# A first scan stage whose normalisation and projections move, pair by pair of time tiles, into the scan's own loop

## The reference, cut to what matters

```python
xn = (x - mu) * jax.lax.rsqrt(var + LN_EPS) * ln_w + ln_b
x_proj = jnp.einsum('bld,ed->ble', xn, in_proj_w)        # 512 outputs
x_ssm, gate = jnp.split(x_proj, 2, axis=-1)              # 256 and 256
A = -jnp.clip(jnp.exp(A_log), -10.0, -0.01)
# each step, for 256 channels x 16 states:
h = jnp.clip(h * A[None] + x_t[:, :, None] * Bm[None], -10.0, 10.0)
y = jnp.einsum('bid,id->bi', h, C)
out = (out_f + out_b) * 0.5 * jax.nn.silu(gate)
return jnp.einsum('bli,di->bld', out, out_proj_w)
```

## Time and profile before

| what | value |
|---|---|
| median of 3 runs | 1257.77 us (1256.69 to 1260.92) |
| time of the profiled execution | 1258.15 us |
| its span | 1256.3 us |
| mean granted TensorE clock | 0.911 |
| VectorE busy over the span | 1009.9 us (80%) |
| TensorE busy over the span | 1027.6 us (82%) |
| ScalarE busy over the span | 714.5 us (57%) |
| GpSimd busy over the span | 582.9 us (46%) |

### The profile page before, as it was taken

One profiled execution on the slowest core, in us unless ns is written; L12 is line 12 of the kernel. 1 busy time (PEld: TensorE's weight loads), 2 busy tenths in 40 slices (PEclk: granted clock), 3 DMA queues, 4 the chain that ended last, 5 costly groups with the idle time before them and its releaser, 6 DMA issues. The chain is left out here.

```text
span 1256.3 us, 22969 instructions
## 1 busy us (share of the span) xinstructions
PE 1027.6 (82%) x8295; PEld 739.2 (59%) x8295; DVE 1009.9 (80%) x2090; ACT 714.5 (57%) x1504; POOL 582.9 (46%) x895
## 2 busy tenths in 40 slices
PE   2999888456599999999999788492688888778696
PEld 1555544143499999999999657340233333536555
DVE  4699999964599888899897537877999999677575
ACT  3866755015466666666665253266677777247453
POOL 2100000002588888888885231010799999225360
PEclk9988988777799999999999979886799999969989
DMA  1000000002211112111100010000200000000001
GB/s 44 1 1 1 2 1 1 1 14 98 89 61 66 69 74 75 71 66 66 71 27 2 1 23 1 1 1 4 61 1 1 0 1 1 1 2 3 3 0 30
DMA packets 16849, 32.49 MB, mean 26 GB/s; under 512 B 5072, under 2 KB 11968, under 8 KB 16736
## 3 DMA queue, kind: packets, MB, share of 16 engines
q1 hardware_dynamic: 16736, 31.02, 7.2%
HBM read 30.10 MB, written 0.92 MB: 25 GB/s over the span
## 5 line engine op out<-in xcount | busy, mean ns | idle before, releaser
L2129 POOL TENSOR_TENSOR m_h_in<-m_dtu,m_bs 128x448 f32<-128x448 f32 x128 | 144.4, 1148 | 69.7 <-DVE m_dtu L2173 53.6
L2196 DVE TENSOR_TENSOR_SCAN m_hs<-msp_da,m_h_in 128x448 f32<-128x448 f32 x128 | 136.4, 1082 | 1.5 <-ACT msp_da L2156 0.8
L672 DVE SCALAR_TENSOR_TENSOR l0r_u<-l0r_u,l0r_a_col 128x1024 f32<-128x1024 f32 x110 | 136.9, 1294 | 0.6 <-ACT l0r_u L627 0.6
L1054 POOL TENSOR_TENSOR bl_sc<-bl_sc,bl_topall 125x1456 f32<-125x1456 f32 x32 | 105.3, 3290 | 59.4 <-ACT bl_topall L1216 59.3
L627 ACT ACTIVATE l0r_u<-l0rp_pu 128x512 f32<-128x512 f32 x224 | 112.0, 643 | 35.9 <-PE l0rp_pu L563 35.8
L2092 PE MATMUL msp_py<-m_hc,ident 128*128 128x448 f32 x256 | 117.2, 542 | 0.0
L766 POOL MEMSET bq_lT<- 128x256 f32 x1 | 0.3, 311 | 238.0 <-POOLq L107 238.0
L563 PE MATMUL l0rp_pu<-l0r_xs,l0r_eb 32*128 32x256 f32 x896 | 104.6, 434 | 4.8 <-ACT l0r_u L627 4.1
L1291 PE MATMUL bl_pS<-b_qw,bl_xcT 128*125 128x112 f32 x768 | 104.0, 278 | 0.0
L2147 ACT ACTIVATE m_bs<-msp_pb 128x448 f32<-128x448 f32 x128 | 69.2, 541 | 44.1 <-PE msp_pb L2076 42.5
L563 PEld LDWEIGHTS l0rp_pu<-l0r_xs,l0r_eb 32*128 32x128 f32 x896 | 71.6, 193 | 37.4 <-ACT l0r_u L627 28.2
(11 more groups left out here) (401 smaller groups left out, 2528.3 us busy)
## 6 DMA issues: line engine op xcount, KB each, us to landing
b_xc<-in_ctx SPq DMA_DIRECT2D x16, 750.0 KB
bl_more<-in_ctx SPq DMA_DIRECT2D x16, 750.0 KB
x_tm<-in_x SPq DMA_DIRECT2D x1, 896.0 KB, 6.0
cw_cT<-in_ctx_headT SPq DMA_DIRECT2D x1, 896.0 KB
out_dram<-x_tm SPq DMA_DIRECT2D x4, 224.0 KB, 2.5
w_up<-in_L_ffn_w SPq DMA_DIRECT2D x1, 512.0 KB, 4.2
w_down<-in_L_ffn_w SPq DMA_DIRECT2D x1, 512.0 KB, 5.4
l0s_win<-in_L_attn_in_proj_wT SPq DMA_DIRECT2D x1, 256.0 KB, 2.6
```

The costliest lines, as they stand in the source:

```text
L672: ve.scalar_tensor_tensor(state(c, i, r), prev, a_col[:, :], state(c, i, r), ALU.mult, ALU.add).then_inc(step_done, 1)
L1054: pool.tensor_tensor(sc[0:KP, n % 3, :, :], sc[0:KP, n % 3, :, :], over(topall[0:KP, n % 2, :].unsqueeze(1), [KP, KT + 1, QR]), ALU.subtra ...
L2129: pool.tensor_tensor(h_in[:, n % NU, :], dtu[:, half, cols], bs[:, n % NU, :], ALU.mult).then_inc(s["db"], 1)
L2196: ve.tensor_tensor_scan(hs[:, n % NU, :], da[:, n % 2, 0:CH], h_in[:, n % NU, :], 0.0, ALU.mult, ALU.add).then_inc(s["scan"], 1)
```

## The change

The input is loaded a second time, as 14 time tiles `xr` whose 128 partitions are four steps times 32 sequences, so that a tile is what a chunk needs. Each of these loads is four DMAs, one for each step of a tile: SP issues tiles 0 and 13 first; ScalarE's queue issues `lnw`, `win` and the other twelve tiles. `x_tm`, needed only by the stage's last part, is loaded behind tiles 0 and 13. The block of constants, the first block of loads, `stage_norm` ahead of the scan and the block of preparations are gone: everything up to the scan's end is one block.

The first pair is normalised on VectorE from statistics of its own. The other twelve tiles get their statistics on VectorE as soon as they are there, one root for all of them on ScalarE (as exp(-0.5 ln)) and a shift on GpSimd; ScalarE then normalises them two tiles at a time. A pair is turned (`turn`), evicted (`take_turned`), projected to `xs` (`project("x", p)`, two matmuls of 256 columns) and kept (`keep`), all through the one PSUM bank `pg`. Pairs 1 to 3 follow the fills of chunks 0 to 2; pairs 4 to 6 follow one a chunk in the loop, and so do the seven pairs of the gate, one a chunk, from chunk 0 on. Every odd fill of chunk 0 is copied by VectorE. B is spread on GpSimd, and the selector is made on ScalarE at chunk 7. The recurrence, the sums and the gating are as before.

The core of the diff, first the order of the loads and of GpSimd's work:

```diff
+            def load_x(eng, tiles, sem):
+                for k in range(TC):
+                    src = d["x"].rearrange("b (j t) d -> t b j d", t=TC)[k]
+                    eng.dma_start(xr[k * B:(k + 1) * B, tiles, :], src[:, tiles, :]).then_inc(sem, 16)
+
+            kept = [("x", p) for p in range(RC + 1)]
+            for c in range(PAIRS):
+                if RC + 1 + c < PAIRS:
+                    kept.append(("x", RC + 1 + c))
+                kept.append(("gate", c))
...
+                @block.sync
+                def _(sp):
+                    sp.dma_start(bcol[:, :, :], d["L0_attn_B_mat"].rearrange("(h p) s -> p h s", p=P)).then_inc(loads_p, 16)
+                    load_x(sp, pair_of_chunks(0), x_first)
+                    sp.dma_start(c_gp[:, 0, :], d["L0_attn_C_mat"].rearrange("(g i) s -> g (i s)", i=CPG)).then_inc(loads_x, 16)
+                    sp.dma_start(c_gp[:, 1, :], d["L0_attn_A_log"].rearrange("(g i) s -> g (i s)", i=CPG)).then_inc(loads_x, 16)
+                    sp.wait_ge(x_first, 16 * TC)
+                    sp.dma_start(wout[:, :, :], d["L0_attn_out_proj_wT"].rearrange("(h p) d -> p h d", p=P)).then_inc(loads_late, 16)
+                    sp.dma_start(core.x_tm[:, :, :], d["x"].rearrange("b t d -> (b t) d")
+                                 .rearrange("(n p) d -> p n d", p=T2)).then_inc(loads_late, 16)
+                    sp.wait_ge(loads_late, 32)
...
+                    pool.wait_ge(s["rstd"], 2)
+                    pool.tensor_tensor(shift[:, REST], mv[:, REST, 0], rstd[:, REST], ALU.mult).then_inc(s["shift"], 1)
+                    pool.wait_ge(s["shift"], 1)
+                    pool.tensor_scalar(shift[:, REST], shift[:, REST], -1.0, None, ALU.mult).then_inc(s["shift"], 1)
+                    pool.wait_ge(s["mine"], 1)
...
+                    pool.wait_ge(s["got"], 1)
+                    for g in range(NG):
+                        at = (g % (RB // CPG)) * CPG
+                        last = pool.tensor_scalar(cexp[:, g, at:at + CPG], mine[:, :], cA[:, 0, g:g + 1], None, ALU.mult)
+                    last.then_inc(s["cexp"], 1)
```

TensorE and the helpers of ScalarE:

```diff
+                    def turn(p):
+                        pe.wait_ge(s["normed"], p + 1)
+                        if p:
+                            pe.wait_ge(s["x_kept"], kept_at("x", p) - 1)
+                        for r in range(2):
+                            last = pe.transpose(pg[:, r * P:(r + 1) * P], xr[:, p if r == 0 else NCH - 1 - p, :], core.ident[:, :])
+                        last.then_inc(s["xturned"], 1)
+
+                    def project(what, p):
+                        if what == "x":
+                            pe.wait_ge(s["xT"], p + 1)
+                        else:
+                            pe.wait_ge(s["x_kept"], kept_at(what, p) - 1)
+                        for h in range(2):
+                            at = (h if what == "x" else 2 + h) * P
+                            last = pe.matmul(pg[:, h * 2 * P:(h + 1) * 2 * P], win[:, at:at + P], xnT[:, pair_of_chunks(p), :],
+                                             start=True, stop=True)
+                        last.then_inc(s["x_made"], 1)
...
+                    for k in range(2):
+                        pe.transpose(pu[:, NPU - 1, k * NG:(k + 1) * NG], c_gp[:, k, :], core.ident[0:NG, 0:NG]).then_inc(s["turned"], 1)
+                    pe.wait_ge(s["eb"], 1)
+                    pe.wait_ge(s["got"], 2)
+                    for c in range(RC):
+                        inputs(c)
+                        turn(c + 1)
+                        project("x", c + 1)
...
+                        ahead = c + RC + 1
+                        if ahead < PAIRS:
+                            turn(ahead)
                         if c + RC < NCH:
                             inputs(c + RC)
-
...
+                        if ahead < PAIRS:
+                            project("x", ahead)
+                        if c < PAIRS:
+                            project("gate", c)
...
+                    act.dma_start(lnw[:, :], d["L0_attn_ln"]).then_inc(loads_w, 16)
+                    act.dma_start(win[:, :], d["L0_attn_in_proj_wT"]).then_inc(loads_w, 16)
+                    load_x(act, REST, x_rest)
+                    load_tables(nc, act, LN_EXP_TABLES)
+
+                    def root(k, tiles):
+                        act.wait_ge(s["moments"], k + 1)
+                        if k == 0:
+                            act.wait_ge(s["const"], 2)
+                        act.activation(rstd[:, tiles], mv[:, tiles, 1], ACT.Ln, bias=core.eps_ln[:, :]).then_inc(s["lnv"], 1)
+                        act.wait_ge(s["lnv"], k + 1)
+                        act.activation(rstd[:, tiles], rstd[:, tiles], ACT.Exp, scale=-0.5).then_inc(s["rstd"], 1)
+
+                    def normalise(p):
+                        act.wait_ge(s["shift"], 2)
+                        for j in (p, NCH - 1 - p):
+                            last = act.activation(xr[:, j, :], xr[:, j, :], ACT.Identity, bias=shift[:, j:j + 1], scale=rstd[:, j:j + 1])
+                        last.then_inc(s["normed"], 1)
+
+                    def take_turned(p):
+                        act.wait_ge(s["xturned"], p + 1)
+                        if p == 0:
+                            act.wait_ge(loads_w, 32)
+                        act.activation(xnT[:, pair_of_chunks(p), :], pg[:, 0:2 * P].rearrange("p (r x) -> p r x", r=2), ACT.Identity,
+                                       bias=lnw[:, 1:2], scale=lnw[:, 0:1]).then_inc(s["xT"], 1)
+
+                    def keep(what, p):
+                        act.wait_ge(s["x_made"], kept_at(what, p))
+                        act.activation((xs if what == "x" else gate)[:, :, pair_of_chunks(p), :],
+                                       pg[:, :].rearrange("p (h r x) -> p h r x", h=2, r=2),
+                                       ACT.Copy if what == "x" else ACT.Silu).then_inc(s["x_kept"], 1)
```

ScalarE's and VectorE's order:

```diff
-                                act.wait_ge(u_made, n + 1)
+                                if c == 0 and gl % 2:
+                                    continue
+                                if c == 0 and w == WAVES // 2 and gl == 0:
+                                    root(1, REST)
+                                    normalise(1)
...
+                    root(0, pair_of_chunks(0))
+                    take_turned(0)
+                    act.wait_ge(s["turned"], 2)
+                    act.activation(cA[:, 0, :], pu[:, NPU - 1, 0:NG], ACT.Copy, scale=0.5).then_inc(s["got"], 1)
+                    act.activation(cA[:, 1, :], pu[:, NPU - 1, NG:2 * NG], ACT.Exp).then_inc(s["got"], 1)
+                    keep("x", 0)
+                    for c in range(RC):
+                        fill(c)
+                        take_turned(c + 1)
+                        normalise(c + 2)
+                        keep("x", c + 1)
                     for c in range(NCH):
                         if c < half_way:
-                            act.wait_ge(y_made, c + 1)
+                            act.wait_ge(s["y_made"], c + 1)
                             act.activation(yT[:, :, pair_of_chunks(c), :],
-                                           py[:, :].rearrange("p (h r x) -> p h r x", h=2, r=2), ACT.Copy).then_inc(y_taken, 1)
+                                           py[:, :].rearrange("p (h r x) -> p h r x", h=2, r=2), ACT.Copy).then_inc(s["y_taken"], 1)
+                        ahead = c + RC + 1
+                        if ahead < PAIRS:
+                            take_turned(ahead)
                         if c + RC < NCH:
                             fill(c + RC)
+                        if ahead < PAIRS:
+                            keep("x", ahead)
+                        if ahead + 1 < PAIRS:
+                            normalise(ahead + 1)
+                        if c < PAIRS:
+                            keep("gate", c)
+                        if c == half_way:
+                            act.activation(core.selector[:, :, :], over(spread[0:P, :].unsqueeze(2), [P, 32, P]), ACT.Copy)
 
                 @block.vector
                 def _(ve):
                     def state(c, i, r):
                         return u[:, c % RC, TC - 1 - i if r else i, r, :]
...
+                    ve.wait_ge(x_first, 16 * TC)
+                    statistics(0, (0, NCH - 1))
+                    ve.wait_ge(s["rstd"], 1)
+                    for j in (0, NCH - 1):
+                        last = ve.tensor_scalar(xr[:, j, :], xr[:, j, :], mv[:, j, 0:1], rstd[:, j:j + 1], ALU.subtract, ALU.mult)
+                    last.then_inc(s["normed"], 1)
+                    ve.wait_ge(x_rest, 16 * TC)
+                    statistics(1, range(1, NCH - 1))
+                    ve.wait_ge(s["got"], 2)
+                    ve.tensor_scalar(cA[:, 1, :], cA[:, 1, :], -0.01, -10.0, ALU.min, ALU.max).then_inc(s["got"], 1)
+                    ve.wait_ge(s["got"], 3)
```

(8 more changed lines are left out.)

## The result

| | before | after |
|---|---|---|
| median of 6 runs each, us | 1257.38 (1256.69 to 1260.92) | 1247.98 (1244.85 to 1251.40) |
| ratio, 95% interval | | 0.9918 [0.9897, 0.9939] |
| profiled execution (span), us | 1258.15 (1256.3) | 1245.21 (1243.5) |

The kernel became faster by 9.4 us, 0.8%, with the sign that was forecast but not the size: 21 us were forecast, and 1247.98 lies 1 us above the range of 1231 to 1247. The profiled execution is one of the faster ones of after. Its difference from that of before is 12.94 us, and this is what the traces can explain.

A forecast was written before the change was run, and what follows sets the result against it. VectorE was taken to bound the scan, so only its 43.31 us head could shrink: 1258.15 - 23.0 (head) + 2.5 (clock stall) - 0.6 (old gap) gave 1237.0 us, range 1231 to 1247.

The forecast's parts named there:

- First fill: 35.33 - 34.17 = 1.16: In the head, after `keep`: chunk 0's first fill takes 1.16 us and is done at 14.1.
- ScalarE copies eight fills at 7.94 / 16 = 0.50 each, 4.0: In the head: ScalarE's half of chunk 0's fills takes 4.0 us; chunk 0 is ready at 20.3.
- 7.95: 31.6. Due 32.3: Before the loop: chunk 1's fills take 7.95 us and end at 31.6, ahead of VectorE's need at 32.3.
- at the full clock VectorE never waits: In the scan: no gaps at full clock; least slack 0.7 us at chunk 1 and 1.5 at chunk 6.
- the relay: Amid chunk 0's fills: ScalarE takes the second root (0.7 us), GpSimd's shift (0.6) and two normalisations (0.9).
- The load: At the head's start: the first tiles land at 6.0 us, between bounds of 4.7 and 8.1.
- The serial line through `pg`: In the loop, chunks 0 to 2: `keep`, gate projection, `sums`, turn and fills in one line, 15.2 us a chunk.
- The sum of 2.5 for its clock: In the loop: one or two of four periods at 1.2 GHz stall VectorE 1.8 to 5.2 us, taken as 2.5.
- a cold TensorE in fill(1): Sign that would prove the forecast wrong: a gap of several us at chunk 1.
- The C products end near 30, hidden by the fills: On GpSimd: the 32 small products of C end near 30 us, before `sums(0)` at 44.
- The head was long: Rival, 12%: late x or the relay delays chunk 0 to 28 us; gain 15.3, time 1245.
- the loop didn't starve VectorE: Rival, 14%, claimed the opposite: waits for `pg` use up the slack and leave 12 us of gaps, time 1246.5.

The follow-up runs named there:

- e1: The kernel after plus 26 useless matmuls on TensorE ahead of the first turn, while it waits for x: 1249.21 us, ratio 0.9921.
- e3: The kernel after with the second root and pair 1's normalisation moved ahead of chunk 0's fills: 1250.51 us, ratio 0.9925.
- e8: e7 with the gate's pairs projected at chunks 3 to 9, pair 6 first, instead of 0 to 6: 1237.55 us, ratio 0.9832.
- e2: e1 plus two or three useless matmuls in each TensorE pause up to chunk 2: 1236.05 to 1261.32 us in ten runs, ratio of six 0.9866.
- e9: e8 without any of the useless warming matmuls: 1242.62 us, ratio 0.9877.
- e4: The kernel after with ScalarE issuing the other twelve tiles only once tiles 0 and 13 have landed: 1254.69 us, ratio 0.9967.
- e5: The kernel after with GpSimd's 32 products of C of 8 columns made as four of 64: 1247.84 us, ratio 0.9913.
- e11: e8 plus 32 small GpSimd products into a tile nobody reads, after chunk 4's first step: 1236.34 us, ratio 0.9817.
- e6: e2 with GpSimd's 32 products of C made as four wide ones: 1242.39 us, ratio 0.9868.
- e7: e6 with the second root and pair 1's normalisation ahead of chunk 0's fills, as in e3: 1238.80 us, ratio 0.9844.

## Why the prediction missed

**The step that failed** is the price of TensorE's work behind its first projection. It stands in two places of the prediction. The first is the head from the first fill to the start, "First fill: 35.33 - 34.17 = 1.16" and "ScalarE copies eight fills at 7.94 / 16 = 0.50 each, 4.0". Both figures are from rows in which TensorE was at 2.4 GHz. It had been at work since 27.60 by then, its first projections had been slow (1.83 and 1.70, then 2.81 for two, against 0.92 for one later), and the trace of before records the rise to full at 33.0, just ahead of the first fill at 34.17. TensorE's timeline of before:

```profile
29.23 1.70 PE L547 MATMUL l0rp_py<-l0s_xnT,l0s_win 128*128 128x448 f32 x2
30.72 2.81 PE L547 MATMUL l0rp_pu<-l0s_xnT,l0s_win 128*128 128x448 f32 x4
```

In the new head it has no such start, and pauses of 0.7 to 1.9 us for ScalarE between most of its parts. I used the slow price for the first projection and the fast one for all behind it. The second place is the loop, "7.95: 31.6. Due 32.3" for fill(1) and "at the full clock VectorE never waits", with a price for the lower clock only on the periods behind fill(2). Counted from the start of the recurrence, fill(1) was to take 31.6 - 20.3 = 11.3 us, and it took 39.70 - 25.07 = 14.6: 3.3 more against a slack of 0.7, which is the gap of 2.52.

| step | counted | measured | differs |
|---|---|---|---|
| first tiles are there | 6.0 | 7.38 | +1.4 |
| from there to `keep`'s end | 6.9 | 14.11 - 7.38 = 6.73 | -0.2 |
| first fill | 1.16 | 16.33 - 14.11 = 2.22 | +1.1 |
| the fills and the relay, to the start | 6.2 | 25.07 - 16.33 = 8.74 | +2.5 |
| gaps in the stream | 2.5 | 6.15 | +3.65 |
| sum | | | +8.4 |

1237.0 + 8.4 is 1245.4, and the profiled execution took 1245.21. The start at 25.07 lies outside the 18.5 to 24 that the prediction allowed the head. That the head's share is TensorE's clock is shown by e1 (-3.8 from statistics to start). The relay is no second share beside it: alone it was worth 1.7 at most (e3), and together with the warm start nothing (13.8 in e8 with both, 13.9 in e1). That the gap before chunk 1 hangs on its clock too is shown by e2, whose profile has none, and for both gaps by e8 against e9: with and without the warming, 0 against 5.5 us of gaps and 5 us of time.

**The load.** It came late by 1.4, within my bounds of 4.7 and 8.1. e4 shows why: 4.95 without the twelve tiles beside it, 7.4 to 8.4 in the other kernels profiled. So the small pieces do not go free of the 768 KB on ScalarE's queue. The rule of the Trainium skill that I weighed (DMA: Bandwidth & Descriptors, "Queues, rings and completion order": rings take turns) is not refuted by this, sharing is what it says; my reading, that it points nearer to the small load's time, was wrong.

**The loop.** The serial line through `pg` was counted nearly right: 15.2 against 14.75. (fill(3) should have stood at 43.0 + 15.2 = 58.2 and not at 57.8, which takes 0.4 from the slacks behind it and changes nothing else.) The sum of 2.5 for its clock was near the gaps that came at chunk 3 and later (3.6 us), but for another reason. I feared 1.2 GHz in the middle of full work, as the earlier trace rows show. It came at 53.5 to 60.4, the tail of the head's cold stretch; from 60 to 160 us the granted clock was 1.00 and the three periods with a pair of x stayed at 14.75. There the rule of the Trainium skill that I had set aside (TensorE: Matmul & The Clock Gate, "What's actually happening": activity releases the throttle) agrees with the trace. In the head it does not: TensorE was busy 13.73 of 16 us between 20 and 36, worked 10.13 us without a pause from 28.31 on, and its instructions still had the long durations. The chunk-1 gap I had named only as a sign that would prove me wrong ("a cold TensorE in fill(1)"), without a price or a chance.

**What cost nothing.** "The C products end near 30, hidden by the fills": they ended at 39.64, and by what e2 shows without that gap (65.3), they were hidden in after only because the gap before chunk 1 let them finish. The 9.03 us behind that, 0.28 each, came from a stretch of before in which VectorE was idle. The work beside it should have been part of that step.

**The rivals.** None took place as told. The head was long, but by 4.8 and not 7.7; the loop didn't starve VectorE; the times I gave for both (1245 and 1246.5) happen to be near the result because two half-sized losses add up. The range allowed each loss, not the two together: both hang for the most part on one cause, TensorE's clock (1.4 of the head's 4.8 are the load), and I had treated them as apart.

**Open.** The median of after is 2.8 above the execution that was profiled, and runs differ by 6.5 us. Two things seen in the profiles could make it, and one profile a kernel can't divide it between them. First, the rest of the program behind the last gating took 1000.0 in after and 999.8 (e5) to 1004.9 (e11) in the experiments, which don't touch it. Second, the clock does not fall alike: e5, whose TensorE does what after's does, had it at full from 18.4 to 21.8 and at the lower level from 66.2 to 76.4, where after had neither, and its gaps were 8.75 instead of 6.15, with one of 2.67 before chunk 4. What decides where it rises and falls from one execution to the next, no run here shows. Why e2's runs split into two groups was seen in one profile of the slower group only; that the others escape the wait for the products is argued, with e6's runs, all below 1248, on its side. e6's late gaps weren't pursued.

## What to carry to other kernels

A duration holds for the state that its engine was in: when a change moves matmuls to the start of a stage or puts pauses between them, price them all with the slow row, and count one cause that hits several steps as one risk. When a gap closes, ask what used it; here small GpSimd operations lived on VectorE's pause, and four wide ones in place of 32 removed the risk. The best kernel of the study is e8 (e11, which only adds idle work, is equal): 1237.55, ratio 0.9832 [0.9817, 0.9847]. It has e7's edits and the later gate, and its scan is 10 us shorter than that of after.

## What was unexpected in the hardware

- TensorE kept the durations of 1.2 GHz from its first instruction at 9.5 us to 50.1, and again from 53.5 to 60.4, while it was busy 86% of 20 to 36 us, in pieces with pauses of 0.7 to 1.9 us. 26 matmuls ahead gave the first 12 us back only (e1: 1.10 at 11.31, 2.07 at 22.23); in e8, with the pauses filled, the clock stayed at full up to 44.4 us (1.13 at 33.00, 2.07 at 44.42).
- The column of the granted clock showed 1.00 up to 50 us of after, where the instructions had nearly twice the duration. This is the view's doing: in every trace of this case the first record is a rise to full (33.0 in before, 50.1 in after, 5.2 in e1), and the stretch ahead of it counts as full. So the mean of 0.926 of that execution is too high. In e1, where the fall at 22.25 is recorded, the column showed 0.50 between 24 and 32.
- A GpSimd operation of 0.30 us takes 3.6 beside an unbroken stream of VectorE, and VectorE isn't slowed.
